# Weight factors read from PSUM in the weighted building stage, half of the late edge-batch copies on VectorE, and four output buffers per edge batch

## What is computed

```python
msgs = feature[edge_src]                                   # layer 0: sum of neighbours, then an MLP
neigh = segment_sum(msgs, edge_dst); h = relu((feature + neigh) @ W1 + b1) @ W2 + b2
q, k, v = nodes @ Wq + bq, nodes @ Wk + bk, nodes @ Wv + bv # layer 1: attention over edges, 8 heads
scores = einsum('ehd,ehd->eh', q[src], k[tgt]) / sqrt(16)
scores = (scores + edges @ We + be) * cons[tgt] + relu(distances @ Wd1 + bd1) @ Wd2 + bd2
w = exp(scores - segment_max(scores)[tgt]); weights = w / segment_sum(w)[tgt]
agg = segment_sum(weights * v[tgt]); out = layernorm(nodes + agg @ Wo + bo) * gamma + beta
agg = segment_sum(x[src]) / max(deg, 1)                    # layer 2: mean of neighbours, two matrices
agg = segment_sum(edge_val * x[edge_col])                  # layer 3: edge-weighted sum, one matrix
```

## Time and profile before

| | us |
|---|---|
| median of 3 executions | 6285.45 |
| lowest, highest | 6275.57, 6294.4 |
| profiled execution, its time | 6270.86 |
| profiled execution, its span | 6268.7 |
| PE busy | 4219.9 (67%) |
| DVE busy | 3516.1 (56%) |
| POOL busy | 2395.1 (38%) |
| ACT busy | 1951.6 (31%) |

### The profile page before, as it was taken

The page is one execution under the profiler, slowest core; times in us unless marked ns, Lnnn a source line. Parts: engine busy times, 40 slices in busy tenths (PEclk is TensorE's granted clock), DMA queues, the critical chain, the costliest instruction groups (busy, mean ns, idle before and its releaser), DMA issues. The chain is left out here.

```text
span 6268.7 us, 91469 instructions
## 1 busy us (share of the span) xinstructions
PE 4219.9 (67%) x26649; PEld 2834.4 (45%) x26650; DVE 3516.1 (56%) x4701; ACT 1951.6 (31%) x3223; POOL 2395.1 (38%) x2303
## 2 busy tenths in 40 slices
PE   3556654549955666666666666666666653799999
PEld 2324332339932333333333333333333332798888
DVE  3313889876654655565655555655555565774000
ACT  2334243556630011112222222333333333664000
POOL 3320179023324544455444444444444423431000
PEclk7777555559976777777877788778787765899999
DMA  7535563336642223333333334434444442567887
GB/s 128 156 122 173 131 226 118 154 155 223 218 136 51 73 80 88 93 103 103 111 108 110 113 113 122 130 117 122 130 123 127 132 165 88 185 223 249 295 300 266
DMA packets 595115, 918.46 MB, mean 147 GB/s; under 512 B 107581, under 2 KB 519571, under 8 KB 575502
## 3 DMA queue, kind: packets, MB, share of 16 engines
q1 hardware_dynamic: 413600, 527.25, 26.0%
q10 hardware_dynamic: 117359, 250.68, 10.9%
q0 software_dynamic: 64032, 139.15, 9.1%
HBM read 611.74 MB, written 314.96 MB: 148 GB/s over the span
## 5 line engine op out<-in xcount | busy, mean ns | idle before, releaser
L2005 POOL DMA_INDIRECT at_qg<-q_d,at_slot x1616 | 1574.0, 974 | 1666.1 <-DVE at_S L2132 1180.4
L997 PE MATMUL bw_ps<-bw_mov,bw_sta 128*128 128x392 bf16 x7056 | 1815.1, 373 | 556.0 <-issue 514.0
L997 PEld LDWEIGHTS bw_ps<-bw_mov,bw_sta 128*128 128x128 bf16 x7056 | 666.0, 106 | 1081.2 <-issue 867.6
L2048 PE MATMUL at_psk<-at_kp,at_hot 128*128 x4848 | 672.5, 244 | 624.6 <-DVE at_qg L2126 305.8
L2048 PEld LDWEIGHTS at_psk<-at_kp,at_hot 128*128 128x128 bf16 x4848 | 463.4, 106 | 1032.9 <-issue 859.7
L2126 DVE TENSOR_TENSOR at_qg<-at_qg,at_psk 128x816 f32<-128x816 f32 (+1 forms) x303 | 274.1, 905 | 1159.0 <-DMA et_dist<-in_edge_weight 1014.3
L1019 ACT COPY xall<-bw_ps 128x392 f32<-128x392 f32 x520 | 252.3, 485 | 1442.6 <-PE bw_ps L997 707.2
L902 PE MATMUL ba_ps<-ba_mov,ba_sta 128*128 128x196 bf16 x2368 | 440.2, 352 | 329.2 <-issue 203.4
L838 DVE TENSOR_TENSOR bw_mov<-bw_ps,late_lo 128x3136 bf16<-128x3136 f16 x294 | 523.7, 1781 | 145.1 <-PE bw_ps L997 72.5
L981 DVE TENSOR_TENSOR bw_sta<-bw_raw,late_kw 128x1024 bf16<-128x1024 bf16 x882 | 554.4, 682 | 0.0
L1604 PE MATMUL at_p3t<-tile,room 128*128 128x256 f32 (+1 forms) x2450 | 525.1, 376 | 4.9 <-ACT room L1166 4.9
(11 more groups left out here) (545 smaller groups left out, 5115.6 us busy)
## 6 DMA issues: line engine op xcount, KB each, us to landing
tile<-adw_d SPq DMA_DIRECT2D x23, 6272.0 KB, 18.7
adw_d<-xall ACTq DMA_DIRECT2D x65, 1568.0 KB
adj_d<-ba_stage ACTq DMA_DIRECT2D x50, 1568.0 KB, 5.2
l0raw<-adj_d SPq DMA_DIRECT2D x50, 1568.0 KB, 6.5
tile<-adj_d SPq DMA_DIRECT2D x50, 1568.0 KB, 6.5
adw_d<-bw_stage ACTq DMA_DIRECT2D x33, 1568.0 KB
at_rel<-rel_d SPq DMA_DIRECT2D x101, 512.0 KB
et_attr<-in_edge_attr SPq DMA_DIRECT2D x48, 1024.0 KB
```

The costliest lines, as they stand in the source:

```text
L997: ins = pe.matmul(self.ps[:, bass.DynSlice(place, WCOL)], self.sta[:, k, u // 2, :, u % 2], self.mov[:, u // 2, :, u % 2], start=False, st ...
L2005: pool.indirect_dma_start(out=qg[:, ring, b, :], out_offset=None, in_=q_d[:, :], in_offset=bass.IndirectOffsetOnAxis(ap=slot[:, ring, b:b ...
L2048: ins = pe.matmul(ps_k[:, at:at + KW], hot[:, par, sum(ROUNDS[:r]) + u, :], kp[:].rearrange("p j k n -> p (j k n)")[:, bass.DynSlice(place ...
```

## The change

Three edits are made.

1. **Weights from PSUM.** A new step `hold` on DVE, once per group and ahead of the third 0 of that group, copies the group's three weight parts (128x36 words of 32 bits, as a bitwise "and" with -1) into spare words of the fifth PSUM bank, in two halves that alternate. The 882 multiplications take their weights from there; `bw_raw`, `bw_mov` and everything else stay. `hold` waits for the multiplication before it (`s_hot`), and the multiplications for `hold` (`s_held`).
2. **Odd copies on DVE.** In batches 20 to 48 the copies of turns 1 and 3 (PSUM bank 1) are made by DVE (`odd_copies`) with a semaphore of their own (`s_trr1`). The copies of batches 20 to 35 stand in DVE's list ahead of the wait for GpSimd's 49 indirect DMAs. The counting work behind that wait is cut into seven pieces of seven columns, one after the copies of each of the batches 36 to 42.
3. **Four output buffers.** `out_e`, `out_d` and their store semaphores have four buffers, one for each slot, in all 49 batches. `read_e` and `read_d` of batch `i` wait for the store of batch `i - 4`.

The diff, cut to its core (the loops of SP and ACT are re-indexed by slot in the same manner where lines are left out):

```diff
+ESHARE = 20
+EXACT = 36
...
+HELD = 3 * 3 * UV // 2
...
+        for i in range(ESHARE, EXACT):
+            edges.odd_copies(i)
         ve.wait_ge(s_exact, 16 * NB)
...
-        for j0, j1 in ((0, 25), (25, NB)):
+        for i, j0 in enumerate(range(0, NB, 7)):
+            j1 = j0 + 7
+            edges.odd_copies(EXACT + i)
             r = inside[:, 0:j1 - j0, :]
             chain(ve.tensor_tensor(r, rows[:, j0:j1, :], nodeid[:, j0:j1].unsqueeze(2).to_broadcast([P, j1 - j0, P]), ALU.is_lt))
             chain(ve.tensor_reduce(some[:, j0:j1], r, AX.X, ALU.add))
         m = chain(ve.scalar_tensor_tensor(out=c.rp[:, 0:NB], in0=full[:], scalar=float(P), in1=some[:], op0=ALU.mult, op1=ALU.add))
+        for i in range(EXACT + NB // 7, EBATCH):
+            edges.odd_copies(i)
...
-        self.out_e, self.out_d = sb("out_e", [P, 2, EG * P]), sb("out_d", [P, 2, 2, P])
+        self.out_e, self.out_d = sb("out_e", [P, ER, EG * P]), sb("out_d", [P, ER, 2, P])
...
-        self.s_ste, self.s_std = ([c.early_sem(f"et_st{n}{k}") for k in range(2)] for n in "ed")
+        self.s_ste, self.s_std = ([c.early_sem(f"et_st{n}{k}") for k in range(ER)] for n in "ed")
...
-        def read_d(i, par, turn):
+        def read_d(i, slot, turn):
             act.wait_ge(self.s_dmm, i + 3)
-            act.wait_ge(self.s_std[par], 16 * turn + 1)
+            act.wait_ge(self.s_std[slot], 16 * turn + 1)
...
-            act.copy(self.attrT[:, par, m, :], self.ps_t[m % 2][:]).then_inc(self.s_trr, 1)
+            act.copy(self.attrT[:, par, m, :], self.ps_t[m % 2][:]).then_inc((self.s_trr, self.s_trr1)[m % 2], 1)
...
             copy(i, 0, par)
-            copy(i, 1, par)
+            if not shared:
+                copy(i, 1, par)
...
+        for lo, hi, shared in ((1, ESHARE // ER, False), (ESHARE // ER, EBATCH // ER, True)):
+            with act.Fori(lo, hi) as i:
+                for k in range(ER):
+                    batch(ER * i + k, k, i, shared=shared)
...
+    def odd_copies(self, i):
+
+        ve = self.nc.vector
+        for m in (1, 3):
+            ve.wait_ge(self.s_tr, EPAIRS * i + m + 1)
+            if m == 1:
+                ve.wait_ge(self.s_emm, i + 1)
+            ve.tensor_copy(self.attrT[:, i % 2, m, :], self.ps_t[1][:]).then_inc(self.s_trr1, 1)
...
-        pe.wait_ge(self.s_trr, EPAIRS * i + m + 1)
+        pe.wait_ge((self.s_trr, self.s_trr1)[m % 2], 2 * i + m // 2 + 1)
...
-        pe.wait_ge(self.s_trr, EPAIRS * i + EPAIRS + 2)
+        pe.wait_ge(self.s_trr, 2 * i + 3)
+        pe.wait_ge(self.s_trr1, 2 * i + 3)
...
+        spare = self.ps[:, WBANKS * 512 + WCOL:WBANKS * 512 + WCOL + 2 * HELD]
+        self.held = spare.bitcast(I32).rearrange("p (h k n) -> p h k n", h=2, k=3)
+        self.weights = spare.bitcast(BF16).rearrange("p (h k n) -> p h k n", h=2, k=3)
...
+    def hold(self, t, par):
+
+        ve, c = self.nc.vector, self.c
+        ve.wait_ge(self.s_hot, t + 1)
+        ve.tensor_scalar(self.held[:, par, :, :], c.kw[:, 1:4, bass.DynSlice(t, 3 * UV)].bitcast(I32), -1, None, ALU.bitwise_and).then_inc(self.s_held, 3 * UV)
...
         ve.wait_ge(self.s_raw, t + UV)
+        ve.wait_ge(self.s_held, t + UV)
         for k in range(3):
-            ins = ve.tensor_tensor(self.sta[:, k, v, :, :], self.raw[:, :, :, :], pairs(c.kw[:, 1 + k, bass.DynSlice(t, UV)]).unsqueeze(2).to_broadcast([P, UV // 2, P, 2]), ALU.mult)
+            ins = ve.tensor_tensor(self.sta[:, k, v, :, :], self.raw[:, :, :, :], pairs(self.weights[:, par, k, third * UV:(third + 1) * UV]).unsqueeze(2).to_broadcast([P, UV // 2, P, 2]), ALU.mult)
...
         def weighted(g, par, third):
-            build.hots((3 * g + third) * UV, slot_of(par, third))
+            if third == 0:
+                build.hold(3 * g * UV, par)
+            build.hots((3 * g + third) * UV, slot_of(par, third), par, third)
```

More of the change, by code:

```diff
@@ L656, in load_last, with store @@
                 sp.dma_start(self.dist[low + n:low + n + 1, slot, chunk // 16, 0:E - lo - n * P], ew[lo + n * P:E].rearrange("(c e) -> c e", c=1)).then_inc(self.s_dist[slot], 16)
-    def store(self, i, par):
+    def store(self, i, slot):
         sp, d = self.nc.sync, self.c.ed_d
@@ L670, in move @@
         if not first:
-            self.store(i - 1, (slot + 1) % 2)
+            self.store(i - 1, (slot - 1) % ER)
         sp.wait_ge(self.s_pick, i + 1)
@@ L688, in last_moves @@
         sp, n = self.nc.sync, EBATCH
-        self.store(n - ER - 2, 1)
+        self.store(n - ER - 2, ER - 1)
         sp.wait_ge(self.s_pick, n - ER)
@@ L694, in last_moves @@
             self.move(n - 1 - ER + k, k, ahead=False)
-        self.store(n - 2, 1)
+        self.store(n - 2, ER - 1)
         self.store(n - 1, 0)
[L697 to L700, removed]
+        for slot in range(ER):
+            turns = len(range(slot, n, ER))
+            sp.wait_ge(self.s_ste[slot], 16 * EPAIRS * turns + 1)
+            sp.wait_ge(self.s_std[slot], 16 * turns + 1)
     def scalar(self):
@@ L726, in copy, with batch @@
                 act.wait_ge(self.s_emm, i + 1)
-            act.copy(self.attrT[:, par, m, :], self.ps_t[m % 2][:]).then_inc(self.s_trr, 1)
-        def batch(i, slot, turn, first=False, last=False):
+            act.copy(self.attrT[:, par, m, :], self.ps_t[m % 2][:]).then_inc((self.s_trr, self.s_trr1)[m % 2], 1)
+        def batch(i, slot, turn, first=False, last=False, shared=False):
             par = slot % 2
             copy(i, 0, par)
-            copy(i, 1, par)
+            if not shared:
+                copy(i, 1, par)
             if not first:
-                read_e(i - 1, 1 - par, turn if par else turn - 1)
+                read_e(i - 1, (slot - 1) % ER, turn if slot else turn - 1)
             copy(i, 2, par)
-            copy(i, 3, par)
-            read_d(i, par, turn)
+            if not shared:
+                copy(i, 3, par)
+            read_d(i, slot, turn)
             if not last:
@@ L741, in scalar @@
         for k in range(ER):
[L742 to L747, removed]
+            batch(k, k, 0, first=k == 0)
+        for lo, hi, shared in ((1, ESHARE // ER, False), (ESHARE // ER, EBATCH // ER, True)):
+            with act.Fori(lo, hi) as i:
+                for k in range(ER):
+                    batch(ER * i + k, k, i, shared=shared)
+        batch(EBATCH - 1, 0, EBATCH // ER, last=True, shared=True)
+        read_e(EBATCH - 1, 0, EBATCH // ER)
+    def odd_copies(self, i):
[5 more added lines that the diff above has]
+            ve.tensor_copy(self.attrT[:, i % 2, m, :], self.ps_t[1][:]).then_inc(self.s_trr1, 1)
     def hidden(self, i, slot, turn, last=False):
@@ L805, in batches @@
             pe.wait_ge(self.s_wz, 8)
-            for q in (self.s_trr, self.s_emm, self.s_dmm):
+            for q in (self.s_emm, self.s_dmm):
                 pe.sem_inc(q, 2)
-            for q in (self.s_re, self.s_rd, self.s_hid):
+            for q in (self.s_trr, self.s_trr1, self.s_re, self.s_rd, self.s_hid):
                 pe.sem_inc(q, 1)
@@ L968, in clear, with hots @@
         self.nc.scalar.activation(window_bank(self.ps, k), self.c.iota2[:].rearrange("p n u -> p (n u)")[:, 0:WCOL], ACT.Copy, scale=0.0).then_inc(self.s_clear, 1)
-    def hots(self, t, u0):
+    def hold(self, t, par):
+        ve, c = self.nc.vector, self.c
+        ve.wait_ge(self.s_hot, t + 1)
+        ve.tensor_scalar(self.held[:, par, :, :], c.kw[:, 1:4, bass.DynSlice(t, 3 * UV)].bitcast(I32), -1, None, ALU.bitwise_and).then_inc(self.s_held, 3 * UV)
+    def hots(self, t, u0, par, third):
         ve, c = self.nc.vector, self.c
```

16 lines of the change are left out of this document (8 added, 8 removed).

## The result

The changed kernel is slower: 6359.11 us (median of 4 executions, 6350.48 to 6364.01) against 6288.06 us for the kernel before beside it, a ratio of 1.0119 (95% interval 1.0105 to 1.0132), +71 us. I had forecast 6269 with a range of 6236 to 6300. The profiled execution took 6350.48 us, the one of before 6270.86: +79.6 us.

| | before | after | difference |
|---|---|---|---|
| first edge stage, start of the last table | 559.90 | 531.68 | -28.2 |
| attention stage, first to last reduction (101) | 1929.4 to 5110.1 | 1903.6 to 5189.2 | +104.9 |

What follows compares the result with a forecast made beforehand. The attention stage, 52% of the span, was taken as set by DVE waiting on a chain that gathers hold up. Terms -18 - 6 - 5 + 1 + 12 = -16 us against 6285.45 gave 6269, range 6236 to 6300.

Steps and rivals of the forecast that it cites:

- Edit 1, what GpSimd gains: Attention stage: gathers may lose their excess length under multiplications; counted at nothing, with a gain of 20 to 44 us possible.
- the sign that the prediction set itself: Attention stage: the forecast is wrong if the period moves by over 0.15 us; over 98 groups each 0.2 makes 20.
- the first part: Attention stage: gathers hold up DVE's release in three groups of four; the fourth's period is some 5 us shorter.
- Rival A: Attention stage: release follows the gathers' end, so shorter gathers give -20 to -44 us more, 6226 to 6250; chance 0.22.
- Rival B: Attention stage: multiplications from PSUM slow by 0.57 us each, three exposed per group, +168 us, about 6440; chance 0.06.
- Four buffers and copies together: First edge stage: three shortened store waits and copies on DVE, -18 - 6 - 5 + 1 us.
- The first wait: Edge stage, batch 2: ACT idles 19.14 us before `read_d` for a store; four buffers give -18 us (-19 to -5).
- copies that I took at +1: Edge stage, late batches: moving copies from ACT to DVE adds 0.05 us for each of 29, +1 us (0 to +3).
- C: Edge stage: loads or SP's queue hold up batches, so the buffers' -29 shrinks to -8, time 6290; chance 0.15.
- D: Edge stage: DVE's copies come late behind counting or slow semaphores, 1 us per batch, +29 us, 6299; chance 0.07.

Runs made afterwards that it cites:

- before_again: The kernel before, unaltered, run again for its profile on a chip of the short kind, where the kernel before takes 4938 to 4989 us.
- after_again: The changed kernel, unaltered, run again on a chip of the short kind: 4880.17 us against 4940.9 for the kernel before, ratio 0.9871.
- hold_only_2: The changed kernel with the multiplications reading weights from SBUF again, `hold` kept, short kind: 4980.85 us against 4945.52 for the kernel before, ratio 1.0069.

## Why the prediction was wrong, step by step

- **The step that failed is "Edit 1, what GpSimd gains".** It saw the delayed gathers, counted their removal at nothing with a gain of up to 44 us as the other bound, and gave no bound on the side of a loss. On the long kind taking the operand from PSUM, which removes them, cost about 100 us (ratios 1.0119 and 0.997 to before, 0.015 x 6288 = 94; by the times themselves, 6359 - 6255 = 104). By the sign that the prediction set itself, a period that moves by more than 0.15 us, it failed: the mean went from 32.45 to 33.56 us.
- **What lay under it** was one sentence in the first part: every fourth group is shorter, its release comes before the series ends. I took that as given and didn't ask what made it so. It held 24 x 4.4 us of good luck, and the trace of before had the clue: the 1.48 us gather in just these groups. My support, a release 22.9 us after the first gather whatever the length of the series, came from the other three groups only, and there it holds: the median is 22.9 in both kernels. The wait itself was for PE's signal, which the trace's semaphore records could have told.
- **Rival A** had the right direction and nearly the right size for the short kind, though by another path (50 us by the gathers' means, from 20 to 44 forecast; GpSimd is the bound there, and DVE has no late release), and the wrong sign for the long one.
- **`hold`** at 0.12 us per group: its step to the next instruction is 0.10 us (L999 at 2166.05, `bw_raw` at 2166.15), hence some 10 us. Right.
- **The multiplications** keep 680 ns with an operand in PSUM. Rival B, and with it the tier table of the Trainium skill ("VectorE: DVE Perf Modes", section "The perf-mode tier table (the rule you actually need)"), which gives such a tensor_tensor the 1x rate, is refuted for these bfloat16 operands.
- **Four buffers and copies together**: -28.2 us at the end of the stage against -28. Right. The first wait gave 17.35 of the 18 forecast. By parts it is less exact: copies that I took at +1 seem to be worth something on the short kind, up to 9 us; on the long kind the parts were not run.
- **C and D** didn't happen.
- **The forecast's own range**, 6255 to 6285, is narrower than the bounds that it names: these add up to -39 and +30 us, 6246 to 6315. The measured 6359 lies outside either.

The delays of single gathers themselves are what the Trainium skill says in "SBUF — State Buffer", section "Who interferes with whom": a VectorE instruction with two SBUF inputs contends with a GpSimd instruction that reads SBUF. All runs agree: the mean gather takes 973 to 1037 ns with both inputs in SBUF, 944 to 960 with one in PSUM. What a removed delay is worth it can't say; here the time went down by some 50 us or up by about 100.

## What to carry to other kernels

When a repeated unit of work has a short variant, find out what makes it short before changing anything near it; a change that makes one engine's work shorter can lengthen the whole where another engine's signal had come through in its gaps (here the operand is shown, the gap only likely). An average (974 to 946 ns per gather) says nothing of which ones matter: look at them by position. And a bound for an unknown needs both sides, above all for something that looks like pure waste.

## What of the hardware was not expected

- On the long kind, PE's signal for round 1 stands in the trace up to 14.7 us after the start of the matmul that carries it, while GpSimd issues gathers back to back (median of groups 8 to 96: 9.0 us before, 10.1 after). In group 8 after, that matmul starts at 2149.23 and the semaphore's record is at 2163.86, 2.8 us after the last gather's end. On the short kind it is 0.24 us at most, in before_again as in after_again, with gathers back to back as well. The three key matmuls take 0.34 us there as on the long kind (before_again at 2800.49, after at 2149.11), so PE's clock at that moment is not the difference. Which path the signal waits for, and why chips differ, no run here shows.
- A gather that starts under three multiplications with two inputs in SBUF can take 2.49 us instead of 0.94, and when both engines have the same period it does so in many groups in a row (54 gathers over 2 us in hold_only_2, 20 of them in 20 series one after the other).
